# The first layer norm and relu of a two-layer graph network made by POOL instead of ScalarE

## What is computed

```
h = max(layernorm(x), 0)
mask = adj > 0
# layer 0, for every graph
r[j, k] = relu((h @ W1a)[j] + (h[j] - h[k]) @ W1b + b1)      # 192 wide
x = x + (sum over k of mask[j, k] * r[j, k]) @ W2 + deg[j] * b2
# layer 1
h = max(layernorm(x), 0)
x = x + (adj @ h) @ W.T
```

## Time and profile before

| | us |
|---|---|
| median of 3 runs | 849.71 |
| lowest and highest | 849.04, 850.85 |
| the profiled execution | 851.92 |
| its span in the trace | 849.9 |
| DVE busy | 820.1 (96%) |
| PE busy | 809.7 (95%) |
| ACT busy | 794.5 (93%) |
| POOL busy | 610.8 (72%) |
| TensorE's granted clock, mean | 0.983 of 2.4 GHz |

### The profile page before, as it was taken

The page is one execution under the profiler, slowest core; times in us unless marked ns, Lnnn a source line. Parts: engine busy times, 40 slices in busy tenths (PEclk is TensorE's granted clock), DMA queues, the critical chain, the costliest instruction groups (busy, mean ns, idle before and its releaser), DMA issues.

```text
span 849.9 us, 26682 instructions
## 1 busy us (share of the span) xinstructions
PE 809.7 (95%) x8242; PEld 712.0 (84%) x8243; DVE 820.1 (96%) x2908; ACT 794.5 (93%) x2241; POOL 610.8 (72%) x1164
## 2 busy tenths in 40 slices
PE   3779999999999999999999999999999999999996
PEld 1447888988898889888988898888888988998884
DVE  6989999999999999999999999999999999999994
ACT  4768999999999999999999999999999999999993
POOL 0855777777787777777777777777777777777773
PEclk9779999999999999999999999999999999999998
DMA  9800000000000000000000000000000000000000
GB/s 336 324 1 2 2 14 20 21 15 20 21 20 9 21 21 18 17 21 21 20 9 21 20 21 15 21 20 20 8 20 21 20 14 21 21 20 9 27 1 23
DMA packets 26704, 27.54 MB, mean 32 GB/s; under 512 B 3520, under 2 KB 24512, under 8 KB 25536
## 3 DMA queue, kind: packets, MB, share of 16 engines
q1 hardware_dynamic: 25488, 25.37, 8.8%
q10 hardware_dynamic: 1072, 0.43, 0.2%
HBM read 21.59 MB, written 4.19 MB: 30 GB/s over the span
## 4 chain that ended last, share of the span: by engine, by line
PE 84%; DVE 6%; issue 3%; ACT 3%; POOL 2%; DMA 1%; SPq 0%; ACTq 0%; POOLq 0%; DVEq 0%
PE ring L400 45%; PE ring L428 8%; PE prep L457 4%; DVE acc L804 4%; PE post L494 3%; PE post L500 3%; PE post L487 3%; PE post L488 3%; PE prep L465 3%; PE prep L468 2%; PE prep L463 2%; PE post L492 2%; POOL rstd L969 1%; DMA x_all<-x_nbf_dram 1%; PE prep L459 1%
## 5 line engine op out<-in xcount | busy, mean ns | idle before, releaser
L804 DVE SCALAR_TENSOR_TENSOR acc<-ring,acc 128x384 f32<-128x384 f32 x896 | 491.7, 549 | 0.6
L561 ACT COPY ring<-P 128x384 f32<-128x384 f32 x1024 | 467.5, 506 | 23.4 <-DVE acc L804 10.4
L400 PE MATMUL ring<-PQ,onehot_space 128*128 128x192 f16 x4096 | 418.7, 247 | 5.5 <-ACT ring L561 2.4
L400 PEld LDWEIGHTS ring<-PQ,onehot_space 128*128 128x128 f16 x4096 | 328.7, 99 | 42.7 <-issue 13.5
L900 POOL TENSOR_SCALAR start<-P,spare 128x192 f32<-128x192 f32 x128 | 131.9, 1030 | 135.5 <-ACT P L611 135.0
L924 POOL TENSOR_TENSOR row_space<-row_space 128x192 f32<-128x192 f32 x256 | 153.3, 599 | 29.7 <-ACT row_space L599 14.0
L790 DVE TENSOR_SCALAR onehot_space<-mask_all 128x512 f16<-128x512 f16 x512 | 161.8, 318 | 0.0
L428 PE MATMUL ring<-PQ,owner 128*128 128x384 f16 (+1 forms) x512 | 94.0, 306 | 0.0
L400 PE MATMUL ring<-PQ,onehot_row 128*128 128x192 f16 x768 | 84.4, 246 | 2.0 <-DVE onehot_row L852 2.0
L599 ACT ACTIVATE row_space<-ring 128x576 f32<-128x576 f32 x128 | 83.1, 649 | 0.7 <-PE ring L400 0.7
L804 DVE SCALAR_TENSOR_TENSOR acc<-ring,start 128x384 f32<-128x384 f32 x128 | 71.2, 556 | 6.8 <-PE ring L400 2.5
(11 more groups left out here) (138 smaller groups left out, 1422.0 us busy)
## 6 DMA issues: line engine op xcount, KB each, us to landing
onehot_space<-adj_kbj_dram SPq DMA_DIRECT2D x8, 1024.0 KB, 17.6
adj_again<-adj_kbj_dram SPq DMA_DIRECT2D x128, 64.0 KB, 2.0
x_all<-x_nbf_dram SPq DMA_DIRECT2D x8, 512.0 KB, 18.4
out_dram<-x_all SPq DMA_DIRECT2D x32, 128.0 KB, 1.9
consts<-consts_dram SPq DMA_DIRECT2D x1, 192.0 KB, 2.5
scratch<-w1a_dram ACTq DMA_DIRECT2D x2, 48.0 KB, 4.4
scratch<-w1b_dram ACTq DMA_DIRECT2D x2, 48.0 KB, 6.9
scratch<-b_dram ACTq DMA_DIRECT2D x1, 96.0 KB, 10.2
```

The lines of the kernel that those rows point to most:

```text
L400: last = nc.tensor.matmul(to, hot(s), parts[:, part, H:2 * H], start=False, stop=(part == 1), skip_group_check=True)
L561: return nc.scalar.copy(slots[to][:, bank_], src.unsqueeze(1).broadcast_to([N, PER_BANK, H]))
L804: return nc.vector.scalar_tensor_tensor(sums, slots[to][:, bank_], 0.0, start[:, :, :] if first else sums, ALU.max, ALU.subtract if first ...
```

## The change

ACT no longer makes h1 (L626 is gone). POOL makes it and its two parts in four instructions of 64 columns:

1. a tensor-scalar, max(x - mean, 0), into `h1[:, 0]` (L935 of the changed kernel);
2. its product with `rstd1` in fp32, into `h1[:, 1]` (L943);
3. the same product written in fp16, which is the first part (L944);
4. the difference of 2 and 3, the second part (L946).

The relu can be taken ahead of the product since `rstd1` is positive. `shift1` isn't needed any more, so L972 and its wait go. Two more waits go: ACT's wait for the norm's numbers ahead of its lead steps, and POOL's wait for h1 ahead of L914. POOL's third and fourth instruction wait on POOL's own results. What runs here is the path with plain numbers for b (`isinstance(b, int)`), which is the one without extra loops over edges.

```diff
--- before.py
+++ after.py
@@ ACT, step @@
-                    if i == 4 and exists(b + 3):
-                        if isinstance(b, int) and b == 0:
-                            act.wait_ge(norm1_ready, GROUPS)
-
-                        if exists(b + 1):
-                            act.wait_ge(transposed, b + 2)
-                        nc.scalar.activation(h1[:, (u + 1) % 2, :], x_all[:, b + 3, :], ACT.Relu, bias=shift1[:, bass.ds(b + 3, 1)],
-                                             scale=rstd1[:, bass.ds(b + 3, 1)]).then_inc(h1_ready, 1)
@@ ACT, prologue @@
-            act.wait_ge(norm1_ready, 1)
             lead(step, hi=-2)
@@ POOL, step @@
-                    wait_apart(pool, h1_ready, b)
                     if exists(b - 4):
                         pool.wait_ge(xb_ready, pairs(b, u, t, -4))
...
                 if exists(b + 3):
 
+                    at = bass.ds(b + 3, 1)
+                    scale = rstd1[:, at].broadcast_to([N, F])
+                    if isinstance(b, int) and b <= 0:
+                        pool.wait_ge(norm1_ready, 1 if b < 0 else GROUPS)
+                    if isinstance(b, int):
+                        nc.gpsimd.tensor_scalar(h1[:, 0, :], x_all[:, b + 3, :], mom[:, 0, at], 0.0, ALU.add, ALU.max).then_inc(h1_ready, 1)
...
                     if exists(b + 1):
                         pool.wait_ge(transposed, b + 2)
                     wait_apart(pool, h1_ready, b + 4)
-                    nc.gpsimd.tensor_scalar(h1_parts[:, (u + 1) % 2, 0, :], h1[:, (u + 1) % 2, :], 1.0, None, ALU.mult).then_inc(h1_part_ready, 1)
-                    pool.wait_ge(h1_part_ready, b + 4)
-                    nc.gpsimd.tensor_tensor(h1_parts[:, (u + 1) % 2, 1, :], h1[:, (u + 1) % 2, :], h1_parts[:, (u + 1) % 2, 0, :],
+                    nc.gpsimd.tensor_tensor(h1[:, 1, :], h1[:, 0, :], scale, ALU.mult)
+                    nc.gpsimd.tensor_tensor(h1_parts[:, (u + 1) % 2, 0, :], h1[:, 0, :], scale, ALU.mult).then_inc(h1_part_ready, 1)
+                    wait_apart(pool, h1_part_ready, b + 4)
+                    nc.gpsimd.tensor_tensor(h1_parts[:, (u + 1) % 2, 1, :], h1[:, 1, :], h1_parts[:, (u + 1) % 2, 0, :],
                                             ALU.subtract).then_inc(h1_split, 1)
@@ POOL, prologue @@
                 nc.gpsimd.tensor_tensor(rstd1[:, b], mom[:, 3, b], half_power[:, :].broadcast_to([N, GROUP * PER_PART]),
-                                        ALU.pow).then_inc(pool_step, 1)
-                pool.wait_ge(pool_step, g + 1)
-                nc.gpsimd.tensor_tensor(shift1[:, b], mom[:, 0, b], rstd1[:, b], ALU.mult).then_inc(norm1_ready, 1)
+                                        ALU.pow).then_inc(norm1_ready, 1)
```

More of the change, by code:

```diff
@@ L102, in gnn_kernel @@
         rstd1 = sb("rstd1", [N, B])
-        shift1 = sb("shift1", [N, B])
         deg = sb("deg", [N, B])
@@ L205, in gnn_kernel @@
         dve_step = sem("dve_step")
-        pool_step = sem("pool_step")
         h1_ready = sem("h1_ready")
+        centred = sem("centred")
         transposed = sem("transposed")
@@ L939, in step @@
                 if exists(b + 3):
+                    at = bass.ds(b + 3, 1)
[4 more added lines that the diff above has]
+                        nc.gpsimd.tensor_scalar(h1[:, 0, :], x_all[:, b + 3, :], mom[:, 0, at], 0.0, ALU.add, ALU.max).then_inc(h1_ready, 1)
+                    else:
+                        nc.gpsimd.tensor_tensor(h1[:, 1, :], x_all[:, b + 3, :], mom[:, 0, at].broadcast_to([N, F]), ALU.add).then_inc(centred, 1)
+                        wait_apart(pool, centred, b + 1 - BODY)
+                        nc.gpsimd.tensor_scalar(h1[:, 0, :], h1[:, 1, :], 0.0, None, ALU.max).then_inc(h1_ready, 1)
                     if exists(b + 1):
```

## The result

The changed kernel takes 881.37 us, median of 4 runs (880.65 to 883.47). The kernel before took 850.17 us beside it (4 runs, 849.04 to 850.85). The ratio is 1.0363, with a 95% interval of 1.0347 to 1.038. So the change costs 31 us. The forecast was 858.5 us with a range up to 873: the sign was right, and the size was off by more than a factor of three.

The account below looks back on a forecast made before the run. DVE was taken to set the pace, with the loop DVE, ACT, PE and back. Terms of 9.6 + 0 - 0.6 = +9 us on a median of 849.7 gave 858.7, taken as 858.5 us, range 846 to 873.

Parts of the forecast that it names:

- What bounds the kernel: Main loop: DVE sets the pace, with the loop DVE, ACT, PE and back; ACT waits for DVE's sums.
- the removed activation: ACT's L626, 461 ns a graph: its removal is worth nothing inside the loop, since DVE ends ACT's wait.
- What POOL gets: POOL's h1 work: tensor-scalar as the old L944, two more products; 0.62 us more a graph, bounds 0.5 and 0.75.
- Term 1: PE's L487 waits for POOL's late row sums (L924) in every second step: 9.6 us, bounds 0 and 22.
- Term 2: POOL's tensor-tensors hold up DVE's tensor-scalars that start under them: 0 us net, bounds -6 and +28.
- L843 is hit every pair: Rival: POOL's L924 starts just ahead of DVE's L843, up to +0.44 us a pair; 868 to 881 us, chance 0.18.
- Phases drift from pair to pair: Argument against L843 being hit every pair: the near tie of L924 and L843 would not always fall alike.
- until about 0.14 us before its end: Hold rule: a POOL tensor-tensor holds a DVE tensor-scalar starting under it until 0.14 us before the POOL instruction ends.
- POOL holds to its very end: Rival: moved L914 and L924 hold L790 and L846 longer, +0.23 us a pair, 15 us, 873 us; chance 0.03.
- Swallowed: Rival: POOL is quicker or steps shift so L487 isn't late; 0 to 3 us, 848 to 853 us, chance 0.2.
- faster: Rival: L790's hit in the second step goes unreplaced, L487 isn't late; 6 to 10 us gained, 839 to 847, chance 0.2.
- Term 3: Prologue: POOL's load runs under L969 and ACT's L626 goes, so the start value comes earlier: -0.6 us, bounds -1.1 and 0.

Follow-up runs that it names:

- e1: Kernel before with ACT's h1 activation left out from graph 4 on, POOL's work unchanged: 851.01 us, ratio 1.0007.
- e4: Changed kernel with plain max(x, 0) as POOL's tensor-scalar, the subtraction of the mean left out: 893.76 us, ratio 1.0509.
- e3: Changed kernel with POOL's four small second-norm instructions moved behind the row sums of an odd step: 870.19 us, ratio 1.0227.
- e2: Kernel before with two unread products of 64 columns more on POOL in each step: 916.64 us, ratio 1.0784.
- e5: Kernel before with two or three one-column tensor-scalars more on POOL per step: 880.36 us (ratio 1.0356) and 894.69 us (1.052).
- v3: Changed kernel, h1 instructions ahead of POOL's wait for P, plus one one-column tensor-scalar in odd steps: 849.15 us, ratio 0.9975; with two 851.57 us, 1.0002.
- v2: Changed kernel with POOL's four h1 instructions moved ahead of its wait for ACT's P and the start value: 855.04 us, ratio 1.0059.
- v1: Kernel before with POOL's four second-norm instructions moved behind the row sums, no work added: 882.03 us, ratio 1.0378.

## Why the prediction was right or wrong

**What bounds the kernel, and the removed activation: right.** e1 measured the relief at a ratio of 1.0007, which is none. In the changed kernel ACT idles 44.8 us ahead of its seeds for DVE. The chain on the page of the kernel before runs through PE for 84% of the span, so DVE leads by little.

**What POOL gets: the tensor-scalar was mis-sized.** I gave the new tensor-scalar the duration of the old L944, "same columns and kind". The kind wasn't the same: two operations and an operand for each partition take 574 ns on the mean, and the next instruction starts 0.71 us after it (340.90 to 341.61) instead of the 0.50 that I took; the plain form of e4 takes 399. From the start of the tensor-scalar to that of L946 it was 0.50 us in the earlier trace rows. Now it is 1.28 us in the one step (335.06 to 336.34) and 1.43 in the other, so +0.78 and +0.93 instead of +0.62, beyond my upper bound of 0.75. POOL's busy time rose by 88.9 us, at the upper end of the 70 to 90. The products themselves were sized rightly (0.29 us).

**Term 1, PE waits for the row sums: the mechanism right, the size half.** 9.6 us were forecast within 0 and 22, and DVE's idle time rose by 18.1. The lateness itself came out, by luck: 0.21 us in each of 64 pairs would be 13.4 us, and PE was late by 0.45 us in every second pair, 13.6 us in all, with 0.78 and 0.93 us added on POOL instead of 0.62. What was mis-sized is how much of it DVE sees. I took 0.15 of 0.21 us. DVE idled 0.86 us behind each wait of 0.46; where the other 0.40 us come from wasn't taken apart. e3, which removes this wait, brings DVE's idle time back to 29.1 us.

**Term 2, DVE and POOL in each other's way: this is the term that failed.** I took 0 and it is +10.8 us of DVE's busy time. I laid one pair of steps over another, found a tie of 0.02 us in the first and a balance in the second, and called that 0. The tie went to POOL about once a pair: L833 was held in 63 of 128 steps, by some 0.15 us each where I had up to 0.44 (9 us in all after 2 before, its mean 304 ns after 249). That is the rival "L843 is hit every pair", whose 868 to 881 us, with term 1 in it, came nearest; the measured time is just above it. By the POOL instruction behind whose end the held ones end, the holds of DVE are, before and after, about 16 and 20 us for the row sums, 2 and 8 for L937 (now L926), 7 and 5 for the start value, 3 and 3 for L917, and under 1 for the four new instructions together. So the new instructions hold almost nothing themselves: they push the old ones onto other instructions of DVE. I had no term for L937 and none for the start value.

"Phases drift from pair to pair" was wrong for the changed kernel, where a pattern of four steps comes back almost without change (the kernel before goes to and fro between a few such patterns). But it isn't the pair that I had laid out with POOL shifted, since a held instruction moves what is behind it on DVE by up to 0.4 us, and PE and ACT follow. Both bounds held by themselves (0 to 22, -6 to +28). I took a low value in each, and the range of the sum ended at 873, while the two upper bounds together make 50 us.

**The rule of the holds.** A held DVE tensor-scalar ends 0.15 us behind the end of POOL's tensor-tensor if it has 512 columns (L790), and 0.05 us behind it if it has 128 (L843, L852). This holds within 0.01 us for the tensor-tensors of 64 to 192 columns in all twelve traces. In e2 the first L853 ends at 326.35 and L938 at 326.30. My "until about 0.14 us before its end" says the same for L790 and L852, whose free times are 0.28 and 0.19 us, and is too late for L843, whose free time is 0.24: 0.19 us. Two parts of the rule were wrong. POOL's tensor-scalars hold too (e3, e5). And not each tensor-tensor does: the power of two columns (L960, 0.73 us) held none of the 361 tensor-scalars that started under it with their own length to spare.

"POOL holds to its very end" followed the Trainium skill's page "SBUF — State Buffer" ("Who interferes with whom"), by which whoever issues first has the shared ports "for the whole instruction". The main point of that page of the Trainium skill, that this lock exists between the two engines and costs time, decides this case; the traces agree on that in each of these kernels. Whether a tensor-tensor holds to its very end can't be told from these runs: a release 0.13 to 0.19 us early, and a lock to the end on a DVE instruction that has already done that much of its work, give the same times. The rival's extra 0.23 us a pair supposed that it had done nothing by then. Under the start value the trace disagrees with "for the whole instruction", since in e3 the second L842 is let go, and the third is free, 0.47 us before L890 ends. The advice of the Trainium skill's page "GPSIMD Engine Reference" ("4.1 Engine selection") against elementwise work on GpSimd fits the 3.6% of the change. It compares with VectorE, though, and here the work came from ACT, and in the order of v3 it cost nothing.

**Swallowed, and faster: didn't come about**, though v2 and v3 show that "swallowed" was possible with the same work in another order (855 us, and 849 with one small instruction more).

**Term 3, the prologue: right.** The start value's first instance starts at 58.41 us instead of 58.90, -0.5 us where -0.6 was forecast:

```profile
52.92 5.49 POOL L969 TENSOR_TENSOR rstd<-mom,half_power 128x32 f32<-128x32 f32 x1
...
58.41 0.94 POOL L890 TENSOR_SCALAR start<-P,spare 128x192 f32<-128x192 f32 x1
```

**What stays open.** The split into 18.1 us of idle time and 10.8 us of holds is a reading of one profiled execution. No experiment takes one of the two away and leaves the other as it is, because each of them moves the phases: e3 removes the idle time and adds 10 us of holds. Why the engines settle into one pattern of hits in one kernel and into another in the next wasn't worked out. Since the patterns repeat over two or four graphs, a forecast would have to follow the instructions of DVE, POOL, PE and ACT over a few graphs until they repeat; nobody has tried it here.

## What to carry to other kernels

Where DVE sets the pace and its small tensor-scalars run beside POOL's tensor-tensors, don't count the added POOL work as a cost alone, but also as a shift of phase: the same amount of work gave 850 or 882 us by its order alone (v1), and more work gave less time (v3). The change of DVE's busy time at an equal count of instructions shows in one number how much more it was held up, and its idle time the rest; read these two ahead of any single line. Then look whether the steps repeat, and over how many: a pair that was read once may be one of two kinds. What helped here was to put the work for POOL in front of one of POOL's own waits (v2), and to start a row sum just behind a DVE tensor-scalar instead of just ahead of it (v3).

## What the runs showed of the hardware

- POOL's small instructions have a price by kind: for 64 columns a product takes 0.29 us (L943), a tensor-scalar with one operation 0.40 (e4), one with two operations and an operand for each partition 0.57 (L935). A tensor-scalar of one column still takes about 0.23 us (v3).
- POOL's tensor-tensors of 64 to 192 columns hold DVE's tensor-scalars. One product of 64 columns, 0.29 us long, costs the DVE instruction that meets it 0.14 us (329 against 186 ns, e2). The power of two columns (L960) holds none.
- POOL's tensor-scalars hold them for a part of their time: one of one column for some 0.09 us (275 against 186 ns for the second L853 of e5), the start value of 192 columns for up to 0.19 us near its beginning and near its end (330 and 367 ns for L842 in e3), and not between.
- DVE's own scalar-tensor-tensor L804 isn't held: its first sums take 544 to 560 ns in all 128 graphs.
- Four instructions of two columns in another place (v1) cost 32 us of 850, and one instruction of one column in every second step (v3) gained 6 to 7 us.
